# Causal attention: the masked row maximum over two PSUM banks in one instruction, and the exponentials one head at a time

## The chip, the cores and the metric

The kernel runs on one core of a Trainium2 chip. The metric is the device time of one execution in microseconds (us). A core has TensorE (PE, matrix multiplies, with its weight loads shown as PEld), VectorE (DVE), ScalarE (ACT), GpSimd (POOL) and SyncE (SP, which here issues DMAs). Each engine takes its own instructions strictly in order, and semaphores hold an engine back until another has counted far enough. TensorE writes to PSUM, which has eight banks; a bank holds 512 float32 values in each of 128 partitions.

## The reference

The program is two "macaron" layers on `x` of 4 sequences x 1024 tokens x 256 channels. Only the attention of the second layer is touched by the change:

```python
q, k, v = split(x @ w_attn.T + b_attn)            # 16 heads of 16 channels
scores = einsum('bhqd,bhkd->bhqk', q, k) / sqrt(16)
scores = where(mask, scores, -inf)                # causal: k <= q; and (odd, odd - 1) is shut out too
w = softmax(scores, axis=-1)
y = einsum('bhqk,bhkd->bhqd', w, v)
return y @ w_proj.T + b_proj
```

The sequence length is 1024, since the stream `x` is drawn as 4 x 1024 x 256. Before it come two FP4 feed-forward layers, a local attention and a mixture of experts; after it another mixture of experts. None of these is touched.

## The kernel before

`causal_attention` works on "quads": four heads of one sequence, 16 quads in all. Query and key are split into three bf16 parts each, so one product has 96 rows of contraction. A quad needs two passes over its scores.

**Pass one, the row maximum.** For each head and each block of 128 queries (`qb`), the scores of all keys up to the diagonal are multiplied (L2203, `max_scores`) and reduced to one negated maximum per row (L2106 and L2110, `reduce_max`). A bank holds 512 keys, so a block with `qb` of 4 or more takes two steps: the first 512 keys go through a plain `tensor_reduce` (L2110), the rest through a custom instruction that adds the mask and takes the minimum (L2106). `MAX_STEPS` lists the 48 steps of a quad, widest block first. The two partial maxima are joined in `split_max` (L2118). The maxima are then split into two bf16 parts, turned by TensorE (L2210, `turn_max`), copied out by DVE (`store_shift`, L2129) and put under the query rows by two DMAs (L2060).

**Pass two, the exponentials.** For each block of 128 keys (`kb`) and each half `Q` of the queries, TensorE multiplies the scores with the maximum already subtracted (L2226) and adds the mask on the diagonal (L2229); ACT takes the exponential (L2183); TensorE multiplies it with the values in float32 (L2243, `values`). `EXP_SLOTS` lists 24 slots of two heads each. Results of a half are copied by ACT (L2175), turned by TensorE (L2254, `turn_y`) and divided on DVE (L2138, L2140).

**PSUM.** Three banks (`RING = 3`) go round between TensorE and DVE for the steps of pass one and the turned results. Four banks from bank 3 on hold two pairs of heads for ACT. Bank 7 collects the values.

**What sets the order.** Everything is written out by hand. Pass one of the next quad is laid between the slots of pass two: `spread` gives each place (before and after the scores of a slot) steps in proportion to the TensorE columns in that place, up to slot 18 of 24. Two waits tie TensorE to the others: a step of pass one waits until the step `RING` places before it has been emptied (L2202), and the scores of slot `s` wait until the exponential of slot `s - 2` is done (L2222). `values` of four heads are issued after the scores of the slot pair that follows.

Of the kernel before, what the change touches and what calls it, by code (L numbers as in the profile page):

```python
# [15 lines left out]
BF16 = mybir.dt.bfloat16  # L16
# [3 lines left out]
ALU = mybir.AluOpType  # L20
ACT = mybir.ActivationFunctionType
AX_X = mybir.AxisListType.X

P = 128
# [1882 lines left out]
def causal_attention(ch, name):  # L1907
# [9 lines left out]
    nc, ps = ch.nc, ch.ps  # L1917
    RING, EXPB, YB = 3, 3, 7
    QUADS = BATCHES * HEADS // QUAD
# [5 lines left out]
    QB = TPB  # L1925
    MAX_STEPS = [(h, qb, k0, min(512, (qb + 1) * P - k0)) for qb in reversed(range(QB)) for h in range(QUAD)
                 for k0 in range(0, (qb + 1) * P, 512)]
    EXP_SLOTS = [(Q, kb, pair) for Q in range(HALVES) for kb in range(4 * Q + 4) for pair in range(2)]
    NM, NE = len(MAX_STEPS), len(EXP_SLOTS)
    MAX_BY, M_AT, Y0_AT, Y1_AT = 18, 19, 13, 3  # L1930
    NPB = 4
    VW = HD + 1
# [4 lines left out]
    def columns(s):  # L1937

        Q, kb, _ = EXP_SLOTS[s]
        n = 512 - max(0, kb - 4 * Q) * P  # L1940
        return 2 * n + (2 * P if kb >= 4 * Q else 0), (4 * n + 512 if s % 2 else 0)

    def spread(slots):

        places = [(s, i) for s in slots for i in range(2)]
        work = [columns(s % NE)[i] for s, i in places]
        share, at = sum(n for _, _, _, n in MAX_STEPS) / sum(work), {p: [] for p in places}
        p, room = 0, work[0] * share
        for k, (_, _, _, n) in enumerate(MAX_STEPS):
            while room < n / 2 and p + 1 < len(places):  # L1950
                p += 1
                room += work[p] * share
            at[places[p]].append(k)
            room -= n
        return at
# [37 lines left out]
    def place(q, what):  # L1993

        return PLACE[q, what], PLACE[q, what] % RING

    with ExitStack() as ctx:
# [35 lines left out]
        nm = ch.sb(name + "nm", [P, 2, QUAD, QB], ctx=until_y_done)  # L2033
        nm2 = ch.sb(name + "nm2", [P, 2, QUAD, QB], ctx=until_y_done)
        mp = ch.sb(name + "mp", [P, 4, QUAD * QB], BF16, ctx=until_y_done)
        mT = ch.sb(name + "mT", [2 * QUAD * QB, P], BF16, ctx=until_y_done)
        E = ch.sb(name + "E", [P, NPB, 2, 512], ctx=until_y_done)
        yT = ch.sb(name + "yT", [P, 512], ctx=until_y_done)
        forbidden = ch.sb(name + "forbidden", [P, 512], BF16, ctx=until_y_done)
        unread = ch.sb(name + "unread", [P, RING, 512], BF16, ctx=until_y_done)  # L2040
        rden = ch.sb(name + "rden", [P, 4, QUAD], ctx=until_y_done)
# [8 lines left out]
        with nc.Block() as block:  # L2050
            @block.sync
            def _(sp):
# [12 lines left out]
                def step(q, t, c, end):  # L2065

                    place_shift(q, c)
                    if not end:
                        sp.wait_ge(pv_ok, q * NE + 4)
                        sp.sem_inc(ch.fence, 1)  # L2070
                        stack(q + 2, (c + 2) % NQ)
# [24 lines left out]
            def _(dve):  # L2096
# [3 lines left out]
                def reduce_max(q, k):  # L2100
                    h, qb, k0, n = MAX_STEPS[k]
                    at, bank = place(q, k)
                    dve.wait_ge(filled, at + 1)
                    dst = (nm if k0 == 0 else nm2)[:, q % 2, h, qb:qb + 1]
                    if k0 + n == (qb + 1) * P:
                        nc.vector.tensor_tensor_reduce(out=unread[:, bank, 0:n], in0=ps[:, bank, 0:n],  # L2106
                                                       in1=forbidden[:, 512 - n:512], scale=-1.0, scalar=-MASKED,
                                                       op0=ALU.add, op1=ALU.min, accum_out=dst).then_inc(emptied, 1)
                    else:
                        nc.vector.tensor_reduce(dst, ps[:, bank, 0:n], AX_X, ALU.max, negate=True  # L2110
                                                ).then_inc(emptied, 1)
                    if k == NM - 1:
                        split_max(q % 2)

                def split_max(u):
                    nc.vector.drain()
                    far = nm[:, u, :, 4:QB]
                    nc.vector.tensor_tensor(far, far, nm2[:, u, :, 4:QB], ALU.min)  # L2118
                    nc.vector.drain()
                    flat = nm[:, u, :, :].rearrange("p h q -> p (h q)")  # L2120
                    nc.vector.tensor_copy(mp[:, 0, :], flat)
                    nc.vector.drain()
                    nc.vector.tensor_tensor(mp[:, 1, :], flat, mp[:, 0, :], ALU.subtract).then_inc(mp_ok, 1)  # L2123
# [22 lines left out]
                nc.vector.drain()  # L2146
                nc.vector.tensor_copy(forbidden[:, 512 - P:512], ch.mask[:, 0, :])
                nc.vector.drain()
# [19 lines left out]
            def _(act):  # L2168
                def store_y(q, Q):
                    act.wait_ge(pv_ok, q * NE + 12 + 16 * Q)  # L2170
                    if Q:
# [5 lines left out]
                def step(q, t, c, end):  # L2177
                    for s, (Q, kb, pair) in enumerate(EXP_SLOTS):
                        n = 512 - max(0, kb - 4 * Q) * P
                        act.wait_ge(s_ok, q * NE + s + 1)  # L2180
                        act.wait_ge(pv_ok, q * NE + s + 1)
                        bank = EXPB + 2 * (s % 2)
                        nc.scalar.activation(E[:, s % NPB, :, 0:n], ps[:, bank:bank + 2, 0:n], ACT.Exp,  # L2183
                                             scale=float(HD) ** -0.5).then_inc(e_ok, 1)
                        if s == 1 and q:
                            store_y(q - 1, 1)
                        if s == 9:
                            store_y(q, 0)
# [4 lines left out]
            def _(pe):  # L2193
                def max_scores(q, k):

                    h, qb, k0, n = MAX_STEPS[k]
                    c = q % NQ
# [3 lines left out]
                    if at >= RING:  # L2201
                        pe.wait_ge(emptied, at - RING + 1)  # L2202
                    nc.tensor.matmul(ps[:, bank, 0:n], Qs[c][0:STACK, h, qb * P:(qb + 1) * P],  # L2203
                                     Ks[c][0:STACK, h, k0:k0 + n], start=True, stop=True).then_inc(filled, 1)

# [8 lines left out]
                def scores(q, c, s):  # L2214
                    Q, kb, pair = EXP_SLOTS[s]
                    q0 = max(kb * P, Q * 512)
# [5 lines left out]
                    pe.wait_ge(e_ok, q * NE + s + 1)  # L2222
                    for hh in range(2):
                        h = 2 * pair + hh
                        o = ps[:, EXPB + 2 * (s % 2) + hh, :]
                        last = nc.tensor.matmul(o[:, 0:n], Ks[c][:, h, kb * P:(kb + 1) * P],  # L2226
                                                Qs[c][:, h, q0:q0 + n], start=True, stop=not diag)
                        if diag:
                            last = nc.tensor.matmul(o[:, 0:P], ch.identb[:, :], ch.mask[:, 1, :],  # L2229
                                                    start=False, stop=True)  # L2230
                    last.then_inc(s_ok, 1)

                def values(q, c, k):

                    Q, kb, _ = EXP_SLOTS[2 * k]
                    off = max(0, kb - 4 * Q) * P
                    if k == 0:
                        pe.wait_ge(va_ok, q + 1)
                    if kb == 0:
                        pe.wait_ge(y_stored, q * 2 + Q + 1)  # L2240
                    pe.wait_ge(e_ok, q * NE + 2 * k + 4)
                    for h in range(QUAD):
                        last = nc.tensor.matmul(ps[h * WIN:(h + 1) * WIN, YB, off:512],  # L2243
                                                Va[:, c, kb, h * VW:h * VW + WIN],
                                                E[:, (2 * k + h // 2) % NPB, h % 2, 0:512 - off],
                                                start=kb == 0, stop=kb == 4 * Q + 3)
                    last.then_inc(pv_ok, 2)

# [10 lines left out]
                pe.sem_inc(y_stored, 1)  # L2259
                pe.sem_inc(pv_ok, 4)  # L2260
                pe.sem_inc(e_ok, 2)
                for k in range(NM):
# [3 lines left out]
                def step(q, t, c, end):  # L2266
                    for s in range(NE):
# [3 lines left out]
                        for j, k in max_steps(q, s, 1):  # L2271
                            max_scores(j, k)
                        if s % 2 and s > 1:
                            values(q, c, (s - 3) // 2)
                        elif s == 1 and q:
                            values(q - 1, (q - 1) % NQ, NE // 2 - 1)
                        if s == Y1_AT and q:
# [5 lines left out]
                turns(pe, step)  # L2283
                values(QUADS - 1, (QUADS - 1) % NQ, NE // 2 - 1)
                turn_y(QUADS - 1, 1)
# [132 lines left out]
```

## Time and profile before

| | us |
|---|---|
| median of 3 runs (2200.66 to 2204.34) | 2203.64 |
| the profiled execution | 2202.5 |
| its span, first to last instruction | 2200.7 |
| TensorE busy in it | 1868.9 (85%) |
| VectorE busy | 1717.7 (78%) |
| ScalarE busy | 1004.6 (46%) |

The causal attention lies between about 1229 and 1754 us of the span. A period of one quad runs from one turning of the maxima (the only instruction of L2210) to the next. The busy time of TensorE counts each matmul with its way through the array, so that matmuls overlap in it; how long one really holds the engine is read from the start of the next.

### The profile page before, as it was taken

To read this page: it belongs to the slowest core of one execution; us is meant where nothing else is said; L and a number is where in the kernel's file an instruction comes from. 1 tells how busy PE (TensorE), PEld (TensorE's weight loads), DVE (VectorE), ACT (ScalarE), POOL (GpSimd) and SP (SyncE) were. 2 spreads that over 40 slices of the span, in tenths; PEclk is the share of its full clock that TensorE was granted. 3 is DMA by queue.
4 is the path that set the end of the run, shared out by engine and by line. 5 is a ranking of instruction groups with operands and counts; after the bars stand their busy time and mean duration, and the time that the engine had idled before them with its cause. 6 is when DMAs were issued, how large, how long until landed. Compare 5 with 4: busy or idle time off the path is not lost. (4 is left out here: it accounts for less than half of the span.)

```text
span 2200.7 us, 36425 instructions
## 1 busy us (share of the span) xinstructions
PE 1868.9 (85%) x11363; PEld 1353.1 (61%) x11363; DVE 1717.7 (78%) x4040; ACT 1004.6 (46%) x1972; POOL 803.7 (37%) x862
## 2 busy tenths in 40 slices
PE   2799997889999539999978799999999874599998
PEld 1777786778777328787856334444444362487787
DVE  8788984598987568777978788888888366787788
ACT  1333334433332814334556256566666635243345
POOL 2223321133332657886244400000000036688843
PEclk7899997999999659999989699999999986699999
DMA  5000001100000622224425524324432016122256
GB/s 187 1 0 0 0 1 23 35 1 0 0 0 1 206 78 86 89 92 125 153 66 157 103 41 59 48 41 59 59 59 31 2 62 202 45 90 90 92 156 189
DMA packets 112048, 150.28 MB, mean 68 GB/s; under 512 B 19431, under 2 KB 84237, under 8 KB 111373
## 3 DMA queue, kind: packets, MB, share of 16 engines
q1 hardware_dynamic: 95232, 106.53, 20.1%
q0 software_dynamic: 14400, 40.41, 5.9%
q8 instruction: 87, 1.43, 0.3%
q10 hardware_dynamic: 2252, 1.29, 0.2%
q14 instruction: 77, 0.62, 0.1%
HBM read 100.71 MB, written 47.20 MB: 67 GB/s over the span
## 5 line engine op out<-in xcount | busy, mean ns | idle before, releaser
L2183 ACT ACTIVATE t_E<-ps 128x1024 f32<-128x1024 f32 (+3 forms) x384 | 292.6, 813 | 217.9 <-PE ps L2229 164.3
L1569 PE MATMUL ps<-m_w,m_xT 128*128 (+1 forms) x1248 | 348.9, 415 | 1.2 <-DVE m_xT L1649 1.2
L2203 PE MATMUL ps<-t_Ks,t_Qs 96*128 96x512 bf16 (+3 forms) x768 | 234.5, 343 | 19.2 <-PEq L1737 5.7
L2106 DVE CUSTOM_DVE_ANT_0 t_unread<-ps,t_forbidden 128x256 bf16<-128x256 f32 (+3 forms) x512 | 233.8, 486 | 21.3 <-PE ps L2203 19.4
L1569 PEld LDWEIGHTS ps<-m_w,m_xT 128*128 128x128 f32 x1248 | 223.5, 192 | 39.4 <-issue 2.0
L693 PE MATMUL ps<-wdT,f_hT 128*128 128x256 f32 (+1 forms) x768 | 193.2, 394 | 18.2 <-ACT f_hT L735 18.2
L2226 PE MATMUL ps<-t_Qs,t_Ks 98*128 98x512 bf16 (+3 forms) x768 | 199.1, 329 | 3.9 <-DMA t_Qs<-t_mT 2.6
L1587 PE MATMUL ps<-m_w,m_hT 128*128 (+1 forms) x1248 | 200.3, 296 | 0.5 <-DVE m_hT L1666 0.5
L2110 DVE TENSOR_REDUCE t_nm<-ps 128x1 f32<-128x512 f32 x256 | 176.4, 689 | 25.4 <-PE ps L2203 23.8
L192 POOL TENSOR_TENSOR f_h<-f_h,f_hs 128x704 f32<-128x704 f32 x64 | 88.7, 1386 | 276.6 <-DVE f_h L230 276.6
L1621 ACT ACTIVATE m_hT<-ps 128x256 fp32r<-128x256 f32 x208 | 80.1, 385 | 227.5 <-PE ps L1578 227.5
L2091 POOL COPY t_Va<-t_V 128x128 f32<-128x128 f32 x64 | 16.1, 295 | 436.9 <-DVE t_mp L2123 436.6
L2203 PEld LDWEIGHTS ps<-t_Ks,t_Qs 96*128 96x128 bf16 x768 | 72.9, 98 | 166.6 <-DVE t_nm L2106 66.8
L693 PEld LDWEIGHTS ps<-wdT,f_hT 128*128 128x128 f32 (+1 forms) x768 | 137.1, 191 | 60.5 <-ACT f_hT L735 25.7
L1656 DVE TENSOR_TENSOR m_ab<-ps,m_b 128x512 f32<-128x512 f32 x208 | 143.1, 688 | 36.5 <-PE ps L1569 35.5
L2243 PE MATMUL ps<-t_E,t_Va 128*32 128x512 f32 (+3 forms) x1536 | 163.8, 498 | 0.0
L1587 PEld LDWEIGHTS ps<-m_w,m_hT 128*128 128x128 f32 x1248 | 162.4, 191 | 0.9 <-DVE m_hT L1666 0.9
L223 ACT ACTIVATE f_hmagic<-f_h 128x704 f32<-128x704 f32 x64 | 50.8, 793 | 240.7 <-DVE f_h L197 240.7
L1485 POOL DMA_INDIRECT m_picked_out<-m_y,m_dst_row x144 | 143.9, 999 | 42.1 <-issue 32.5
L1475 POOL DMA_INDIRECT m_xg<-m_rows,m_src_row x144 | 140.1, 973 | 50.7 <-issue 34.8
L657 PE MATMUL ps<-wgT,f_xT 128*128 128x352 f32 x768 | 145.5, 340 | 7.4 <-DVE f_h L565 4.5
L657 PEld LDWEIGHTS ps<-wgT,f_xT 128*128 128x128 f32 x768 | 128.0, 197 | 13.7 <-DVE f_xT L558 5.7
(299 smaller groups left out, 3900.2 us busy)
## 6 DMA issues: line engine op xcount, KB each, us to landing
m_raw<-in_L_ffn_rw SPq DMA_DIRECT2D x48, 256.0 KB, 3.2
t_parts<-t_qkv_part SPq DMA_DIRECT2D x64, 192.0 KB, 2.7
t_Qs<-t_parts SPq DMA_DIRECT2D x96, 128.0 KB, 4.1
t_Ks<-t_parts SPq DMA_DIRECT2D x96, 128.0 KB, 6.8
m_yl<-m_picked_out SPq DMA_DIRECT2D x40, 256.0 KB, 3.1
m_rows<-m_xn SPq DMA_DIRECT2D x16, 512.0 KB, 4.2
m_xg<-m_rows SPq DMA_DIRECT2D x64, 128.0 KB, 2.7
m_y<-m_picked_out SPq DMA_DIRECT2D x24, 256.0 KB, 3.1
```

The lines of the kernel that those rows point to most:

```text
L657: last = nc.tensor.matmul(ps[:, bank + half, 0:FH], xT[:, par, kx, c, j * P:(j + 1) * P], w[:, kw, c, half * FH:(half + 1) * FH], start=k ...
L693: last = nc.tensor.matmul(ps[:, DOWN, 0:D], hT[0:rr, r, :], ch.wdT[0:rr, r, :], start=r == 0, stop=r == FC - 1)
L1485: nc.gpsimd.indirect_dma_start(out=picked_out[:, :], out_offset=bass.IndirectOffsetOnAxis(ap=dst_row[:, i:i + 1], axis=0), in_=y[:, i % RI ...
L1569: last = nc.tensor.matmul(ps[:, H1 + u, :], xT[:, u, kx, k, :], of_expert(w1, kw, e, k), start=n == 0, stop=n == 3 * DC - 1)
L1587: last = nc.tensor.matmul(ps[:, OUT + u, 0:D], hT[:, u, kh, f, :], of_expert(w2, kw, e, f), start=n == 0, stop=n == 3 * FK - 1)
L1656: tt(ab[:, u, :], ps[:, H1 + u, :], row_of(b1, e), ALU.add).then_inc(ab_ok, 1)
L2106: nc.vector.tensor_tensor_reduce(out=unread[:, bank, 0:n], in0=ps[:, bank, 0:n], in1=forbidden[:, 512 - n:512], scale=-1.0, scalar=-MASKED ...
L2110: nc.vector.tensor_reduce(dst, ps[:, bank, 0:n], AX_X, ALU.max, negate=True).then_inc(emptied, 1)
L2183: nc.scalar.activation(E[:, s % NPB, :, 0:n], ps[:, bank:bank + 2, 0:n], ACT.Exp, scale=float(HD) ** -0.5).then_inc(e_ok, 1)
L2203: nc.tensor.matmul(ps[:, bank, 0:n], Qs[c][0:STACK, h, qb * P:(qb + 1) * P], Ks[c][0:STACK, h, k0:k0 + n], start=True, stop=True).then_inc ...
L2226: last = nc.tensor.matmul(o[:, 0:n], Ks[c][:, h, kb * P:(kb + 1) * P], Qs[c][:, h, q0:q0 + n], start=True, stop=not diag)
L2243: last = nc.tensor.matmul(ps[h * WIN:(h + 1) * WIN, YB, off:512], Va[:, c, kb, h * VW:h * VW + WIN], E[:, (2 * k + h // 2) % NPB, h % 2, 0 ...
```

## The change

Pass one: a block of queries is one step, 32 in a quad. For `qb` of 4 or more two matmuls fill two neighbouring banks, and one masked instruction reads both. The plain reduction, `nm2` and the joining of partial maxima go. `RING` is 2, each place two banks wide. Pass two: a slot is one head, 48 in a quad, in three single banks (`NEB = 3`); scores of slot `s` wait for the exponential of slot `s - 3`. `values` of heads 4k to 4k+3 come after the scores of slot 4k + 6. The number of exponential buffers stays the same in heads (8).

```diff
-    RING, EXPB, YB = 3, 3, 7
+    RING, EXPB, NEB, YB = 2, 4, 3, 7
-    MAX_STEPS = [(h, qb, k0, min(512, (qb + 1) * P - k0)) for qb in reversed(range(QB)) for h in range(QUAD)
-                 for k0 in range(0, (qb + 1) * P, 512)]
-    EXP_SLOTS = [(Q, kb, pair) for Q in range(HALVES) for kb in range(4 * Q + 4) for pair in range(2)]
+    MAX_STEPS = [(h, qb) for qb in reversed(range(QB)) for h in range(QUAD)]
+    EXP_SLOTS = [(Q, kb, h) for Q in range(HALVES) for kb in range(4 * Q + 4) for h in range(QUAD)]
-    MAX_BY, M_AT, Y0_AT, Y1_AT = 18, 19, 13, 3
-    NPB = 4
+    MAX_BY, M_AT, Y0_AT, Y1_AT = 36, 39, 26, 8
+    NPB = 2 * QUAD
+    LAG = QUAD + 2
...
-        return PLACE[q, what], PLACE[q, what] % RING
+        return PLACE[q, what], 2 * (PLACE[q, what] % RING)
+    def wide(bank, n):
+        return ps[:, bank:bank + 2, :].rearrange("p b n -> p (b n)")[:, 0:n]
...
-                    if k0 + n == (qb + 1) * P:
-                        nc.vector.tensor_tensor_reduce(out=unread[:, bank, 0:n], in0=ps[:, bank, 0:n],
-                                                       in1=forbidden[:, 512 - n:512], scale=-1.0, scalar=-MASKED,
-                                                       op0=ALU.add, op1=ALU.min, accum_out=dst).then_inc(emptied, 1)
-                    else:
-                        nc.vector.tensor_reduce(dst, ps[:, bank, 0:n], AX_X, ALU.max, negate=True
-                                                ).then_inc(emptied, 1)
+                    nc.vector.tensor_tensor_reduce(out=unread[:, at % RING, 0:n], in0=wide(bank, n),
+                                                   in1=forbidden[:, SEQ - n:SEQ], scale=-1.0, scalar=-MASKED,
+                                                   op0=ALU.add, op1=ALU.min, accum_out=nm[:, q % 2, h, qb:qb + 1]
+                                                   ).then_inc(emptied, 1)
...
-                    far = nm[:, u, :, 4:QB]
-                    nc.vector.tensor_tensor(far, far, nm2[:, u, :, 4:QB], ALU.min)
-                    nc.vector.drain()
...
-                        nc.scalar.activation(E[:, s % NPB, :, 0:n], ps[:, bank:bank + 2, 0:n], ACT.Exp,
+                        nc.scalar.activation(E[:, s % NPB, 0:n], ps[:, EXPB + s % NEB, 0:n], ACT.Exp,
                                              scale=float(HD) ** -0.5).then_inc(e_ok, 1)
...
-                    nc.tensor.matmul(ps[:, bank, 0:n], Qs[c][0:STACK, h, qb * P:(qb + 1) * P],
-                                     Ks[c][0:STACK, h, k0:k0 + n], start=True, stop=True).then_inc(filled, 1)
+                    for k0 in range(0, (qb + 1) * P, 512):
+                        n = min(512, (qb + 1) * P - k0)
+                        last = nc.tensor.matmul(ps[:, bank + k0 // 512, 0:n], Qs[c][0:STACK, h, qb * P:(qb + 1) * P],
+                                                Ks[c][0:STACK, h, k0:k0 + n], start=True, stop=True)
+                    last.then_inc(filled, 1)
...
-                    pe.wait_ge(e_ok, q * NE + 2 * k + 4)
+                    pe.wait_ge(e_ok, q * NE + QUAD * k + QUAD + NEB)
...
-                        if s % 2 and s > 1:
-                            values(q, c, (s - 3) // 2)
+                        if s % QUAD == LAG % QUAD and s >= LAG:
+                            values(q, c, (s - LAG) // QUAD)
-                pe.sem_inc(e_ok, 2)
+                pe.sem_inc(e_ok, NEB)
```

Two places show what moves on TensorE. The first is the group of key block 3 in the first half, where a head has 128 query columns. Before (L2226 and L2229 scores and mask, L2203 a step of pass one, L2243 values; in brackets the semaphores waited for, `t_exp` from ACT, `t_emptied` from DVE):

```order
L2226 MATMUL ps<-t_Qs,t_Ks 128x128 [waits t_exp]
L2229 MATMUL ps<-maskb,identb 128x128
L2226 MATMUL ps<-t_Qs,t_Ks 128x128
L2229 MATMUL ps<-maskb,identb 128x128
L2203 MATMUL ps<-t_Ks,t_Qs 128x512 [waits t_emptied]
L2226 MATMUL ps<-t_Qs,t_Ks 128x128 [waits t_exp]
L2229 MATMUL ps<-maskb,identb 128x128
L2226 MATMUL ps<-t_Qs,t_Ks 128x128
L2229 MATMUL ps<-maskb,identb 128x128
L2203 MATMUL ps<-t_Ks,t_Qs 128x256 [waits t_emptied]
L2243 MATMUL ps<-t_E,t_Va 32x256 [waits t_exp]
L2243 MATMUL ps<-t_E,t_Va 32x256 x3
```

The same place in the changed kernel (the lines are now 2224, 2227, 2202 and 2241); the first head of the group that lies between two runs of values is the last one of 256 columns:

```order
L2224 MATMUL ps<-t_Qs,t_Ks 128x256 [waits t_exp]
L2227 MATMUL ps<-maskb,identb 128x128
L2224 MATMUL ps<-t_Qs,t_Ks 128x128 [waits t_exp]
L2227 MATMUL ps<-maskb,identb 128x128
L2224 MATMUL ps<-t_Qs,t_Ks 128x128 [waits t_exp]
L2227 MATMUL ps<-maskb,identb 128x128
L2224 MATMUL ps<-t_Qs,t_Ks 128x128 [waits t_exp]
L2227 MATMUL ps<-maskb,identb 128x128
L2202 MATMUL ps<-t_Ks,t_Qs 128x512 [waits t_emptied]
L2202 MATMUL ps<-t_Ks,t_Qs 128x256
L2241 MATMUL ps<-t_E,t_Va 32x256 [waits t_exp]
L2241 MATMUL ps<-t_E,t_Va 32x256 x3
```

Each head now has a wait of its own, the four heads stand in a row without a step of pass one between them, and the step is one of 768 columns behind the scores.

The second place is the end of a quad's pass one, where the narrow blocks come, ahead of the values of key block 3 in the second half. Before:

```order
L2226 MATMUL ps<-t_Qs,t_Ks 128x512 [waits t_exp]
L2229 MATMUL ps<-maskb,identb 128x128
L2226 MATMUL ps<-t_Qs,t_Ks 128x512
L2229 MATMUL ps<-maskb,identb 128x128
L2203 MATMUL ps<-t_Ks,t_Qs 128x256 [waits t_emptied] x2
L2226 MATMUL ps<-t_Qs,t_Ks 128x512 [waits t_exp]
L2229 MATMUL ps<-maskb,identb 128x128
L2226 MATMUL ps<-t_Qs,t_Ks 128x512
L2229 MATMUL ps<-maskb,identb 128x128
L2203 MATMUL ps<-t_Ks,t_Qs 128x256 [waits t_emptied] x2
L2203 MATMUL ps<-t_Ks,t_Qs 128x128 [waits t_emptied] x4
L2243 MATMUL ps<-t_E,t_Va 32x512 [waits t_exp]
```

The same place in the changed kernel:

```order
L2202 MATMUL ps<-t_Ks,t_Qs 128x384 [waits t_emptied]
L2224 MATMUL ps<-t_Qs,t_Ks 128x512 [waits t_exp]
L2227 MATMUL ps<-maskb,identb 128x128
L2202 MATMUL ps<-t_Ks,t_Qs 128x256 [waits t_emptied]
L2224 MATMUL ps<-t_Qs,t_Ks 128x512 [waits t_exp]
L2227 MATMUL ps<-maskb,identb 128x128
L2202 MATMUL ps<-t_Ks,t_Qs 128x256 [waits t_emptied] x3
L2202 MATMUL ps<-t_Ks,t_Qs 128x128 [waits t_emptied] x2
L2241 MATMUL ps<-t_E,t_Va 32x512 [waits t_exp]
L2241 MATMUL ps<-t_E,t_Va 32x512 x3
L2202 MATMUL ps<-t_Ks,t_Qs 128x128 [waits t_emptied] x2
```

Six narrow steps stood in a row ahead of the values; now five do, and two more come behind the values. Each of them waits for the step two places before it instead of three.

## Rows read from the trace of the kernel before

**Rows 1.** Windows: us, busy PE, PEld, DVE, ACT, POOL (instructions), clock, DMA share, GB/s

```profile
1229.00:1260.00 31.00, 23.96 (x53) 5.54 (x54) 27.60 (x88) 1.28 (x1) 14.10 (x12) 0.50 0.39 57
...
1292.48:1726.20 433.72, 424.71 (x3263) 181.27 (x3260) 366.07 (x1228) 266.10 (x364) 13.05 (x52) 1.00 0.34 49
```

**Rows 2.** Waits, 1260 to 1726 us: who waited for whom, us, times, longest

```profile
PEld ps L2203 <- DVE t_nm L2106: 57.8, 139, 0.8
PEld ps L2226 <- ACT t_E L2183: 8.7, 14, 0.6
```

**Rows 3.** Timeline, PE: start, us, instruction; two turnings of the maxima

```profile
1292.48 0.23 PE L2210 MATMUL ps<-identb,t_mp 128*128 128x128 bf16 x1
...
1726.20 0.23 PE L2210 MATMUL ps<-identb,t_mp 128*128 128x128 bf16 x1
```

**Rows 4.** Timeline, PE, 1431 to 1444 us: the places where steps wait

```profile
1431.11 0.42 PE L2243 MATMUL ps<-t_E,t_Va 128*32 128x128 f32 x8
...
1431.64 0.23 PE L2203 MATMUL ps<-t_Ks,t_Qs 96*128 96x128 bf16 x1
...
1432.80 0.43 PE L2203 MATMUL ps<-t_Ks,t_Qs 96*128 96x128 bf16 x2
...
1433.39 0.23 PE L2203 MATMUL ps<-t_Ks,t_Qs 96*128 96x128 bf16 x1 [0.16 <-DVE t_nm L2110]
...
1439.02 0.87 PE L2203 MATMUL ps<-t_Ks,t_Qs 96*128 96x384 bf16 x3
...
1439.83 0.64 PE L2243 MATMUL ps<-t_E,t_Va 128*32 128x512 f32 x4
...
1442.33 0.60 PE L2203 MATMUL ps<-t_Ks,t_Qs 96*128 96x256 bf16 x3
...
1443.84 1.07 PE L2243 MATMUL ps<-t_E,t_Va 128*32 128x512 f32 x8
```

**Rows 5.** Timeline, DVE and PEld, pass one of the first quad

```profile
1232.44 0.69 DVE L2110 TENSOR_REDUCE t_nm<-ps 128x1 f32<-128x512 f32 x1
...
1233.05 0.68 DVE L2106 CUSTOM_DVE_ANT_0 t_unread<-ps,t_forbidden 128x512 bf16<-128x512 f32 x1
...
1233.66 0.69 DVE L2110 TENSOR_REDUCE t_nm<-ps 128x1 f32<-128x512 f32 x1
...
1233.80 0.10 PEld L2203 LDWEIGHTS ps<-t_Ks,t_Qs 96*128 96x128 bf16 x1 [0.50 <-DVE t_nm L2106]
...
1254.32 0.29 DVE L2106 CUSTOM_DVE_ANT_0 t_unread<-ps,t_forbidden 128x128 bf16<-128x128 f32 x1
...
1254.53 0.29 DVE L2106 CUSTOM_DVE_ANT_0 t_unread<-ps,t_forbidden 128x128 bf16<-128x128 f32 x1
```

**Rows 6.** Timeline, PE and DVE, 1438 to 1446 us: steps filled, a half divided

```profile
1438.14 0.26 DVE L2138 RECIPROCAL t_rden<-ps 128x16 f32<-128x16 f32 x1 [0.43 <-PE ps L2254]
...
1438.81 0.68 DVE L2106 CUSTOM_DVE_ANT_0 t_unread<-ps,t_forbidden 128x512 bf16<-128x512 f32 x1
...
1443.33 0.29 DVE L2106 CUSTOM_DVE_ANT_0 t_unread<-ps,t_forbidden 128x128 bf16<-128x128 f32 x1
...
1444.84 0.39 PE L2203 MATMUL ps<-t_Ks,t_Qs 96*128 96x512 bf16 x1
...
1445.27 0.69 DVE L2110 TENSOR_REDUCE t_nm<-ps 128x1 f32<-128x512 f32 x1 [0.22 <-PE ps L2203]
```

**Rows 7.** Timeline, PE and ACT, the last quad

```profile
1736.71 1.04 PE L2226 MATMUL ps<-t_Qs,t_Ks 98*128 98x512 bf16 x4
...
1737.36 1.94 ACT L2183 ACTIVATE t_E<-ps 128x1024 f32<-128x1024 f32 x2 [0.68 <-PE ps L2226]
...
1739.35 0.61 PE L2226 MATMUL ps<-t_Qs,t_Ks 98*128 98x512 bf16 x2 [0.31 <-ACT t_E L2183]
```

**Rows 8.** Groups by line and shape, 1260 to 1726 us: busy, mean ns, idle before

```profile
L2183 ACT ACTIVATE t_E<-ps 128x512 f32<-128x512 f32 x58 | 31.5, 595 | 38.3 <-PE ps L2229 38.3
...
L2183 ACT ACTIVATE t_E<-ps 128x256 f32<-128x256 f32 x58 | 20.6, 382 | 23.1 <-PE ps L2229 22.1
```

More of the change, by code:

```diff
@@ L1940, in columns @@
         n = 512 - max(0, kb - 4 * Q) * P
-        return 2 * n + (2 * P if kb >= 4 * Q else 0), (4 * n + 512 if s % 2 else 0)
+        return n + (P if kb >= 4 * Q else 0), (4 * n + 512 if s % QUAD == LAG % QUAD else 0)
     def spread(slots):
@@ L1946, in spread @@
         work = [columns(s % NE)[i] for s, i in places]
-        share, at = sum(n for _, _, _, n in MAX_STEPS) / sum(work), {p: [] for p in places}
+        share, at = sum((qb + 1) * P for _, qb in MAX_STEPS) / sum(work), {p: [] for p in places}
         p, room = 0, work[0] * share
-        for k, (_, _, _, n) in enumerate(MAX_STEPS):
+        for k, (_, qb) in enumerate(MAX_STEPS):
+            n = (qb + 1) * P
             while room < n / 2 and p + 1 < len(places):
@@ L2033, in causal_attention @@
         nm = ch.sb(name + "nm", [P, 2, QUAD, QB], ctx=until_y_done)
-        nm2 = ch.sb(name + "nm2", [P, 2, QUAD, QB], ctx=until_y_done)
         mp = ch.sb(name + "mp", [P, 4, QUAD * QB], BF16, ctx=until_y_done)
         mT = ch.sb(name + "mT", [2 * QUAD * QB, P], BF16, ctx=until_y_done)
-        E = ch.sb(name + "E", [P, NPB, 2, 512], ctx=until_y_done)
+        E = ch.sb(name + "E", [P, NPB, 512], ctx=until_y_done)
         yT = ch.sb(name + "yT", [P, 512], ctx=until_y_done)
-        forbidden = ch.sb(name + "forbidden", [P, 512], BF16, ctx=until_y_done)
-        unread = ch.sb(name + "unread", [P, RING, 512], BF16, ctx=until_y_done)
+        forbidden = ch.sb(name + "forbidden", [P, SEQ], BF16, ctx=until_y_done)
+        unread = ch.sb(name + "unread", [P, RING, SEQ], BF16, ctx=until_y_done)
         rden = ch.sb(name + "rden", [P, 4, QUAD], ctx=until_y_done)
@@ L2068, in step @@
                     if not end:
-                        sp.wait_ge(pv_ok, q * NE + 4)
+                        sp.wait_ge(pv_ok, q * NE + NPB)
                         sp.sem_inc(ch.fence, 1)
@@ L2100, in reduce_max @@
                 def reduce_max(q, k):
-                    h, qb, k0, n = MAX_STEPS[k]
+                    h, qb = MAX_STEPS[k]
+                    n = (qb + 1) * P
                     at, bank = place(q, k)
                     dve.wait_ge(filled, at + 1)
-                    dst = (nm if k0 == 0 else nm2)[:, q % 2, h, qb:qb + 1]
-                    if k0 + n == (qb + 1) * P:
-                        nc.vector.tensor_tensor_reduce(out=unread[:, bank, 0:n], in0=ps[:, bank, 0:n],
-                                                       in1=forbidden[:, 512 - n:512], scale=-1.0, scalar=-MASKED,
-                                                       op0=ALU.add, op1=ALU.min, accum_out=dst).then_inc(emptied, 1)
-                    else:
-                        nc.vector.tensor_reduce(dst, ps[:, bank, 0:n], AX_X, ALU.max, negate=True
-                                                ).then_inc(emptied, 1)
+                    nc.vector.tensor_tensor_reduce(out=unread[:, at % RING, 0:n], in0=wide(bank, n),
+                                                   in1=forbidden[:, SEQ - n:SEQ], scale=-1.0, scalar=-MASKED,
+                                                   op0=ALU.add, op1=ALU.min, accum_out=nm[:, q % 2, h, qb:qb + 1]
+                                                   ).then_inc(emptied, 1)
                     if k == NM - 1:
@@ L2146, in _ @@
                 nc.vector.drain()
-                nc.vector.tensor_copy(forbidden[:, 512 - P:512], ch.mask[:, 0, :])
+                nc.vector.tensor_copy(forbidden[:, SEQ - P:SEQ], ch.mask[:, 0, :])
                 nc.vector.drain()
@@ L2169, in store_y @@
                 def store_y(q, Q):
-                    act.wait_ge(pv_ok, q * NE + 12 + 16 * Q)
+                    act.wait_ge(pv_ok, q * NE + NPB + 4 * QUAD + 8 * QUAD * Q)
                     if Q:
@@ L2177, in step @@
                 def step(q, t, c, end):
-                    for s, (Q, kb, pair) in enumerate(EXP_SLOTS):
+                    for s, (Q, kb, _) in enumerate(EXP_SLOTS):
                         n = 512 - max(0, kb - 4 * Q) * P
@@ L2181, in step @@
                         act.wait_ge(pv_ok, q * NE + s + 1)
-                        bank = EXPB + 2 * (s % 2)
-                        nc.scalar.activation(E[:, s % NPB, :, 0:n], ps[:, bank:bank + 2, 0:n], ACT.Exp,
+                        nc.scalar.activation(E[:, s % NPB, 0:n], ps[:, EXPB + s % NEB, 0:n], ACT.Exp,
                                              scale=float(HD) ** -0.5).then_inc(e_ok, 1)
-                        if s == 1 and q:
+                        if s == 3 and q:
                             store_y(q - 1, 1)
-                        if s == 9:
+                        if s == 3 * QUAD + LAG + 1:
                             store_y(q, 0)
@@ L2194, in max_scores @@
                 def max_scores(q, k):
-                    h, qb, k0, n = MAX_STEPS[k]
+                    h, qb = MAX_STEPS[k]
                     c = q % NQ
@@ L2214, in scores @@
                 def scores(q, c, s):
-                    Q, kb, pair = EXP_SLOTS[s]
+                    Q, kb, h = EXP_SLOTS[s]
                     q0 = max(kb * P, Q * 512)
@@ L2222, in scores @@
                     pe.wait_ge(e_ok, q * NE + s + 1)
[L2223 to L2230, printed above, removed]
+                    o = ps[:, EXPB + s % NEB, :]
+                    last = nc.tensor.matmul(o[:, 0:n], Ks[c][:, h, kb * P:(kb + 1) * P],
+                                            Qs[c][:, h, q0:q0 + n], start=True, stop=not diag)
+                    if diag:
+                        last = nc.tensor.matmul(o[:, 0:P], ch.identb[:, :], ch.mask[:, 1, :],
+                                                start=False, stop=True)
                     last.then_inc(s_ok, 1)
                 def values(q, c, k):
-                    Q, kb, _ = EXP_SLOTS[2 * k]
+                    Q, kb, _ = EXP_SLOTS[QUAD * k]
                     off = max(0, kb - 4 * Q) * P
@@ L2244, in values @@
                                                 Va[:, c, kb, h * VW:h * VW + WIN],
-                                                E[:, (2 * k + h // 2) % NPB, h % 2, 0:512 - off],
+                                                E[:, (QUAD * k + h) % NPB, 0:512 - off],
                                                 start=kb == 0, stop=kb == 4 * Q + 3)
-                    last.then_inc(pv_ok, 2)
+                    last.then_inc(pv_ok, QUAD)
                 def turn_y(q, Q):
@@ L2259, in _ @@
                 pe.sem_inc(y_stored, 1)
-                pe.sem_inc(pv_ok, 4)
-                pe.sem_inc(e_ok, 2)
+                pe.sem_inc(pv_ok, NPB)
+                pe.sem_inc(e_ok, NEB)
                 for k in range(NM):
@@ L2272, in step @@
                             max_scores(j, k)
-                        if s % 2 and s > 1:
-                            values(q, c, (s - 3) // 2)
-                        elif s == 1 and q:
-                            values(q - 1, (q - 1) % NQ, NE // 2 - 1)
+                        if s % QUAD == LAG % QUAD and s >= LAG:
+                            values(q, c, (s - LAG) // QUAD)
+                        elif s == LAG % QUAD and q:
+                            values(q - 1, (q - 1) % NQ, NE // QUAD - 1)
                         if s == Y1_AT and q:
@@ L2283, in _ @@
                 turns(pe, step)
-                values(QUADS - 1, (QUADS - 1) % NQ, NE // 2 - 1)
+                values(QUADS - 1, (QUADS - 1) % NQ, NE // QUAD - 1)
                 turn_y(QUADS - 1, 1)
```

## The prediction

> **What bounds the kernel now.** I read the windows first, then the waits, then the timeline of TensorE. In the steady stretch (1292 to 1726 us) the clock is full, TensorE shows 425 busy us of 434 and VectorE 366 [rows 1]. Fourteen quads pass between the two turnings, 433.72 us, so a quad takes 30.98 us [rows 3]. The reader should not trust the 98%: the real hold of a matmul is columns divided by 2.4 per ns, since starts in a row lie that far apart. The waits view shows whom TensorE waits for: its steps of pass one wait 139 times for the masked instruction of DVE, its scores only 14 times for ACT [rows 2]. Put against the columns, four places of a quad are real stalls [rows 4]. From 1442.33 to 1443.84 two steps of 256 and four of 128 columns stream 0.43 us and the change to float32 values takes 0.10, so 0.98 is waiting; 1432.80 to 1433.39 holds 0.27 of streaming, 0.32 waiting; 1439.02 to 1439.83 holds 0.48 + 0.10, 0.23 waiting; values of 128 columns take 0.36 and the next step starts 0.53 later, 0.17 waiting. Together 1.70 us; the other 29.3 us of a quad are TensorE's own work. The bound is TensorE, plus a hand-over to DVE.
>
> **Numbers for the hand-over.** A DVE read of 512 columns gives way to the next after 0.61 us in both forms, one of 128 after 0.21 [rows 5]: 0.08 us fixed and 1.04 ns a column. TensorE starts 0.14 us after the read that it waited for [rows 5]. A step of 512 streams 0.21 us and is read 0.43 us after its start, so 0.22 us pass between stream and reader [rows 6]. With these figures the traced cluster comes out: its first step of 128 is read from 1443.33 [rows 6], ends 1443.54, the fourth, three places on, starts 0.14 later at 1443.68, and 0.05 + 0.10 us later values begin: 1443.83, traced 1443.84 [rows 4]. For ACT: two matmuls of 512 from 1736.71 end at 1737.14 and the exponential starts at 1737.36, again 0.22; the two exponentials end at 1739.30 and the score that waited starts at 1739.35 [rows 7]. An exponential of 512 elements takes 0.595 us, of 256 0.38 [rows 8]; by that line 0.49 for 384 and 0.28 for 128. A masked block adds 0.06 us of TensorE.
>
> **What goes.** TensorE multiplies the same columns. DVE loses 16 reads a quad at 0.08 us fixed, 1.2 us, and the joining of the maxima, about 0.2. Those are worth something only where TensorE waits for DVE. Wide reads are not in the trace: by the line 1024 columns take 1.14, 896 1.01, 768 0.88, 640 0.74. At worst they cost what two reads do (1.22 for 1024), at best the fixed part is free (1.06); I take the line, since 128 to 512 lie on it.
>
> **What comes on the ACT side.** Behind a waiting score stand all of TensorE's later work and so DVE's steps. The fourth head after a run of values now needs the exponential of the first head after it, where before it needed a head four back, which was done during the values. From the start of the first to the start of the fourth must pass: stream, 0.22, exponential, 0.05.
> - First head 256 columns, then three of 128 (twice a quad): 0.17 + 0.22 + 0.38 + 0.05 = 0.81 needed, TensorE has 0.17 + 0.12 + 0.12 = 0.41. Stall 0.40, twice.
> - Masked 512, then three of 384 (first half): 0.28 + 0.22 + 0.60 + 0.05 = 1.15, against 0.74. Stall 0.41.
> - 384, the turning of the maxima, three of 256 (second half): 0.98 against 0.63. Stall 0.35.
> - Four of 512 with a step of 640 between (twice): 1.08 against 0.94. Stall 0.14, twice.
>
> In the other groups a wide step or a turning stands between and covers it. Sum 1.84 us, near zero before.
>
> **What comes on the DVE side.** A step now waits for the one two places back. In units of the wide steps: stream, 0.22, read, 0.14 must fit between a step and the next but one.
> - Behind the turning of the maxima: 0.43 + 0.22 + 1.14 + 0.14 = 1.93, and TensorE, its ACT wait included, has 1.59. Stall 0.35.
> - A turned half takes one of the two places. Step 7 (896 columns): 0.37 + 0.22 + 1.01 + 0.14 = 1.74, TensorE has 1.43 up to the step behind the turning. Stall 0.3. For the other half DVE divides for 0.67 us [rows 6] and three steps behind it wait 0.2, 0.15 and 0.45: 0.8.
> - The last steps of 640 and first of 512: 0.1.
> - The narrow cluster. Let the first 256 start at 0; the last 384 is read until 0.41. The first 256 is read 0.41 to 0.75. The second starts at 0.41 + 0.14 = 0.55, is there at 0.88 and read until 1.22; the third starts 0.89, read until 1.56; the fourth starts 1.36, read until 2.03; the first 128 starts 1.70, read until 2.24; the second starts 2.17, and values at 2.33. Without waits TensorE would be there at 0.91: stall 1.4 against 0.98 before. It is worse although DVE does the same reads, because two places leave DVE idle while TensorE refills.
>
> Sum 2.95 against 1.70. The old waits at 1431 to 1440 do go; the new ones are dearer.
>
> **Sum.** A quad gains 1.84 + 2.95 - 1.70 = 3.1 us. Fourteen steady quads 43.4, the first, between the other two kinds, 3. Pass one of the first quad runs at a granted clock of 0.50, the level of 1.2 GHz, bound by DVE [rows 1]: the reads save 1.2 and the joining 0.2, but with two places the loop of two steps is 0.14 + columns/1.2 + 0.22 + read, which passes two reads at every width, by 0.04 (1024) to 0.13 us (128) a step; four heads times 0.65 is 2.6. Net +1.1. The last quad has no steps; its groups lengthen by 0.1 to 0.4 and one gets shorter: +1. Together 48.5. The profiled execution took 2202.5 us, 1.1 below the median of the runs, so 2251 by its own time and 2252 beside the median.
>
> Two ideas of the skill pull apart here. The Trainium skill, Advanced Engine Details and Errata, TRN2 Errata (The Read-Write Bubble), advises tiles of 512 or 1024 elements, as ScalarE and VectorE pay a latency between instructions; by it DVE's side gets cheaper and ACT's dearer. The rows agree on the size: 0.08 us a read. The Trainium skill, Perfetto Trace Analysis, Optimization Strategy, reads a gap that repeats on the engine that should be full as too few buffers; by it, going from three places to two and from four heads to three makes the time rise, which is my forecast. The sum above needs neither sentence.
>
> **Rivals.**
> 1. *The saved reads pay (faster).* DVE is busy 84% of the steady stretch [rows 1] and TensorE waits for it; with 1.4 us less a quad and wide steps TensorE would find its place free. If all old waits go and none come: 15 x 1.70 + 1.4 = 27, 2175. Against: the hand-over of a wide step is longer than the work between. It decides if a quad's waits end below 1.70. Chance 0.08. The errata rule above, taken alone, asks for this one.
> 2. *Only the ring costs.* If one-bank exponentials come back soon enough: 1.25 x 15 + 2 = 21, 2224. Against: each needed time is made of traced durations. 0.15.
> 3. *Only the exponentials cost*, the wider steps paying for the lost place: 1.84 x 15 + 1 = 29, 2232. 0.07.
> 4. *Wide reads at the price of two, in places where TensorE waits*: another 1.2 a quad, 2270. 0.12.
> 5. Nothing moves, as losses and gains cancel: 2204. 0.03.
>
> That the change misses its aim in the code is out: the order shows the steps as described.
>
> **How the numbers follow.** My case has 0.55, own range 2240 to 2262. Within 0.2% (about 4.4 us) no change can be told. Slower is my case and rivals 2 to 4: 0.89; same 0.03; faster 0.08. The range from 2222 to 2272 leaves out rivals 1 and 5 and the edges of 2 and 4, under 0.2.
>
> **What would show it.** The period between turnings should be 34 us, not 31. Scores should wait for ACT six times a quad, 0.1 to 0.4 us. Steps behind a turning and in the narrow cluster should wait for DVE, 1.4 us in the cluster. DVE's busy time should fall by more than 1 us a quad and ACT's rise, TensorE's clock stay full. A period of 31 or less, or scores without waits, makes me wrong.

## The result, and the profile after

The changed kernel takes 2254.49 us (median of 4 runs, 2253.16 to 2256.36) against 2202.15 us of the kernel before, run beside it: a ratio of 1.023 with a 95% interval of 1.0218 to 1.0241. The forecast was 2252 us. The profiled execution took 2253.16 us with a span of 2251.4.

The answer to [rows 3], the turnings of the maxima on TensorE's timeline (start in us, duration, instruction):

```profile
1258.34 0.29 PE L2210 MATMUL ps<-identb,t_mp 128*128 128x128 bf16 x1 [0.93 <-DVE t_mp L2121]
...
1294.58 0.22 PE L2210 MATMUL ps<-identb,t_mp 128*128 128x128 bf16 x1
...
1773.59 0.22 PE L2210 MATMUL ps<-identb,t_mp 128*128 128x128 bf16 x1
```

Fourteen quads pass between the last two: 479.01 us, so 34.21 a quad against 30.98. That is 45.3 us of the 50.7 by which the span grew. The windows of these stretches answer to [rows 1] (us, busy PE, PEld, DVE, ACT, POOL, clock, DMA share, GB/s):

```profile
1229.00:1260.00 31.00, 21.00 (x49) 4.01 (x49) 27.01 (x70) 1.28 (x1) 14.29 (x12) 0.50 0.34 51
...
1294.58:1773.59 479.01, 448.44 (x3261) 170.75 (x3260) 351.17 (x992) 297.95 (x700) 13.08 (x52) 1.00 0.32 44
```

The clock of the steady stretch is full as before. DVE's busy time fell from 26.1 to 25.1 us a quad (84% of it before, 73% now); ACT's rose from 19.0 to 21.3, which in the longer quad is 62% after 61%. Neither is at its limit. What grew is waiting. The waits view, 1296 to 1770 us, answers to [rows 2] (who waited for whom, us in total, times, longest):

```profile
PEld ps L2202 <- DVE t_nm L2109: 75.3, 180, 0.8
PEld ps L2224 <- ACT t_E L2180: 70.3, 152, 0.8
```

Scores waited 14 times for ACT before; now 152 times. These figures still contain time in which TensorE streamed something older. To take that out, each matmul's columns/2.4 ns (and 0.10 us more ahead of values) were subtracted, as in the prediction, from the time between its start and the start of the next; what is left was summed over a quad (median of nine quads). Below this is called "by the starts". Before: steps 1.65 us, scores 0. After: steps 2.91, scores 1.83, together 4.74. The difference, 3.09, is nearly all of the 3.23 us by which the quad grew.

The group of the first diff place shows the wait for ACT, on the timeline of TensorE and ACT:

```profile
1468.29 0.28 PE L2224 MATMUL ps<-t_Qs,t_Ks 98*128 98x256 bf16 x1
...
1468.59 0.22 PE L2224 MATMUL ps<-t_Qs,t_Ks 98*128 98x128 bf16 x1
1468.65 0.22 PE L2227 MATMUL ps<-maskb,identb 128*128 128x128 bf16 x1
1468.67 1.04 ACT L2180 ACTIVATE t_E<-ps 128x256 f32<-128x256 f32 x4 [1.45 <-PE ps L2227]
...
1469.11 0.23 PE L2224 MATMUL ps<-t_Qs,t_Ks 98*128 98x128 bf16 x1 [0.24 <-ACT t_E L2180]
```

The first head of 256 columns starts at 1468.29, the fourth of the group at 1469.11: 0.82 us, where 0.81 was worked out. The third head's mask began at 1468.65 and took 0.06, so 0.40 us were lost.

The narrow cluster (the steps of 256 and 128 columns at the end of a quad's pass one), in answer to the last two of [rows 4], on the timeline of TensorE:

```profile
1493.36 0.27 PE L2202 MATMUL ps<-t_Ks,t_Qs 96*128 96x256 bf16 x1
...
1493.90 0.63 PE L2202 MATMUL ps<-t_Ks,t_Qs 96*128 96x256 bf16 x2
...
1494.71 0.57 PE L2202 MATMUL ps<-t_Ks,t_Qs 96*128 96x256 bf16 x2 [0.18 <-DVE t_nm L2109]
...
1495.52 0.23 PE L2202 MATMUL ps<-t_Ks,t_Qs 96*128 96x128 bf16 x1 [0.23 <-DVE t_nm L2109]
...
1495.68 1.07 PE L2241 MATMUL ps<-t_E,t_Va 128*32 128x512 f32 x8
```

From the first 256 to the values 2.32 us pass; the working gave 2.33, of which 1.4 is waiting.

### The profile page after: what moved, and what is told of

It reads as the page before. It is cut to its first block and busy times, and to the rows that moved or that the text cites. A ratio compares the mean times of both kernels' runs of the same rounds, so it can differ in the third digit from the quotient of the medians.

```text
span 2251.4 us, 36905 instructions
## 1 busy us (share of the span) xinstructions
PE 1890.9 (84%) x11363; PEld 1337.8 (59%) x11363; DVE 1704.5 (76%) x3768; ACT 1040.5 (46%) x2356; POOL 804.2 (36%) x862
## 3 DMA queue, kind: packets, MB, share of 16 engines
q10 hardware_dynamic: 2252, 1.29, 0.2%
## 5 line engine op out<-in xcount | busy, mean ns | idle before, releaser
L2109 DVE CUSTOM_DVE_ANT_0 t_unread<-ps,t_forbidden 128x256 bf16<-128x256 f32 (+7 forms) x512 | 372.3, 756 | 123.5 <-PE ps L2202 117.1
L2180 ACT ACTIVATE t_E<-ps 128x512 f32<-128x512 f32 (+3 forms) x768 | 328.4, 494 | 232.2 <-PE ps L2227 173.8
L2202 PE MATMUL ps<-t_Ks,t_Qs 96*128 96x512 bf16 (+3 forms) x768 | 215.0, 342 | 31.6 <-DVE t_nm L2109 23.1
L2224 PE MATMUL ps<-t_Qs,t_Ks 98*128 98x512 bf16 (+3 forms) x768 | 214.0, 331 | 18.4 <-ACT t_E L2180 14.9
L2224 PEld LDWEIGHTS ps<-t_Qs,t_Ks 98*128 98x128 bf16 x768 | 72.8, 97 | 148.5 <-ACT t_E L2180 91.5
L2202 PEld LDWEIGHTS ps<-t_Ks,t_Qs 96*128 96x128 bf16 x768 | 63.0, 98 | 159.9 <-DVE t_nm L2109 105.6
```

What stands on the lines that cost most here:

```text
L2109: nc.vector.tensor_tensor_reduce(out=unread[:, at % RING, 0:n], in0=wide(bank, n), in1=forbidden[:, SEQ - n:SEQ], scale=-1.0, scalar=-MASK ...
L2180: nc.scalar.activation(E[:, s % NPB, 0:n], ps[:, EXPB + s % NEB, 0:n], ACT.Exp, scale=float(HD) ** -0.5).then_inc(e_ok, 1)
L2202: last = nc.tensor.matmul(ps[:, bank + k0 // 512, 0:n], Qs[c][0:STACK, h, qb * P:(qb + 1) * P], Ks[c][0:STACK, h, k0:k0 + n], start=True, ...
```

## The experiments

**The exponential half alone, three banks.** Pass one is that of the kernel before (three places, steps of at most 512), pass two that of the changed kernel:

```diff
-    RING, EXPB, YB = 3, 3, 7
+    RING, EXPB, NEB, YB = 3, 3, 3, 7
...
-    EXP_SLOTS = [(Q, kb, pair) ... for pair in range(2)]
+    EXP_SLOTS = [(Q, kb, h) ... for h in range(QUAD)]
...
```

> The exponential half of the change alone: one head a slot in three banks, while pass one stays as before (steps of at most 512 columns, three places). Theory (the fourth head after the values waits for the exponential of the first, about 2.0 us a quad, and the ring of three keeps its 1.7): a quad takes 33.0 to 33.3 us instead of 31.0, the kernel 2230 to 2236 us. Rival (the loss is all in the ring of two places): 2200 to 2208 us.

2227.69 us, ratio 1.011 (1.0086 to 1.0134); a quad takes 32.50 us:

```profile
1615.13 0.22 PE L2210 MATMUL ps<-identb,t_mp 128*128 128x128 bf16 x1
...
1647.63 0.22 PE L2210 MATMUL ps<-identb,t_mp 128*128 128x128 bf16 x1
```

The rival falls, but the expected size was some 0.6 us a quad too high. By the starts, scores wait 1.38 us a quad and steps 1.55. In three groups, of 256 and 128 columns, the waits are 0.13, 0.19 and 0.19 us instead of the 0.35, 0.41 and 0.41 of the changed kernel. With 48 steps instead of 32, a step of 512 columns stands between the heads of each of these groups, where the changed kernel has none, and each wait is shorter by 0.22 us, about what such a step streams (0.21). So the price of three banks depends on what stands between the heads. The other half of the change alone, wide steps with pairs of heads, was not run: it would take four banks, four banks and the one for the values, nine where there are eight.

**The same with four banks.** One number:

```diff
-    RING, EXPB, NEB, YB = 3, 3, 3, 7
+    RING, EXPB, NEB, YB = 3, 3, 4, 7
```

> As the run with three banks for single heads, but with four (the eighth bank is free when pass one keeps three): the same 768 exponentials, one place more. Theory (depth is what counts): the waits of scores for ACT nearly vanish, a quad takes 30.8 to 31.3 us, 2198 to 2208 us. Rival (twice the number of exponentials is what costs, by its fixed part on ACT): as slow as with three banks, about 2230 us or more.

2208.09 us, ratio 1.002 (1.0009 to 1.0031); a quad takes 31.23 us:

```profile
1602.75 0.22 PE L2210 MATMUL ps<-identb,t_mp 128*128 128x128 bf16 x1
...
1633.98 0.22 PE L2210 MATMUL ps<-identb,t_mp 128*128 128x128 bf16 x1
```

Scores wait no longer (0 us by the starts). So 768 exponentials instead of 384 cost 0.2% and the missing fourth head some 20 us more: the depth is what costs.

**The changed kernel with its four banks given out by the bank.** A wide step takes two, a narrow one or a turned result one; the wait is for the last user of the bank:

```diff
-        return PLACE[q, what], 2 * (PLACE[q, what] % RING)
+        return PLACE[q, what], BANK[PLACE[q, what]]
...
-                    if at >= RING:
-                        pe.wait_ge(emptied, at - RING + 1)
+                    if BEFORE[at] >= 0:
+                        pe.wait_ge(emptied, BEFORE[at] + 1)
...
```

> The changed kernel with its four banks of pass one given out by the bank: a step of more than 512 columns takes two neighbouring ones, every other step and every turned result takes one, so narrow steps are four deep. Theory: the narrow cluster's waits fall from 1.4 to about 0.5 us, the three waits behind the second turned half go (0.6), those behind the turning of the maxima and behind the first turned half stay; 1.5 us a quad, 2229 to 2236 us. Rival (the wide reads themselves are what TensorE waits for, not the number of places): within 5 us of the changed kernel, 2250 to 2255 us.

2227.83 us, ratio to before 1.0104 (1.0079 to 1.013), some 27 us below the changed kernel and a little below the expected 2229; a quad takes 32.65 us:

```profile
1590.10 0.22 PE L2225 MATMUL ps<-identb,t_mp 128*128 128x128 bf16 x1
...
1622.75 0.22 PE L2225 MATMUL ps<-identb,t_mp 128*128 128x128 bf16 x1
```

Waits of steps fall from 2.91 to 1.22 us: in the cluster to 0.42, behind the second turned half to nothing, while those behind the turning of the maxima (0.34) and the first turned half (0.40) stay as expected. Scores still wait 1.97. The number of places explains the step side: the wide reads are still there, and all but 1.22 us of the waits are not.

**Two places, nothing else.** The kernel before with one number changed:

```diff
-    RING, EXPB, YB = 3, 3, 7
+    RING, EXPB, YB = 2, 3, 7
```

> The kernel before with RING = 2 and nothing else: single-bank steps of at most 512 columns, two places. Theory: two places leave DVE idle while TensorE refills in the narrow cluster and behind every turned result; at least the 1.2 us a quad that the ring costs the changed kernel, 2222 to 2250 us. Rival (two places are enough, since DVE's reads take longer than a refill): 2202 to 2208 us.

2269.24 us, ratio 1.0291 (1.0264 to 1.0317). The direction is as expected, the time lies 19 us above the expected range; a quad takes 34.69 us:

```profile
1621.63 0.23 PE L2210 MATMUL ps<-identb,t_mp 128*128 128x128 bf16 x1
...
1656.32 0.23 PE L2210 MATMUL ps<-identb,t_mp 128*128 128x128 bf16 x1
```

Steps wait 5.24 us. Some 13 of the 65 us fall in the first quad and its pass one, the rest in the steady quads. The 1.2 us that I had taken from the changed kernel is a net figure: there the wide instruction has paid a part back, as the next run shows. With narrow steps the lost place by itself is dearer than the whole change.

**The changed kernel without the wide instruction.** Single heads in three banks, two places, steps of at most 512. Against the first experiment one number differs:

```diff
-    RING, EXPB, NEB, YB = 3, 3, 3, 7
+    RING, EXPB, NEB, YB = 2, 3, 3, 7
```

> The changed kernel without the wide instruction: one head a slot in three banks, two places, but steps of at most 512 columns in single banks as before (the plain and the masked form). It tells what merging two reads is worth by itself. Theory (a wide step gives DVE more work for each hand-over, so two places leave it less idle): slower than the changed kernel; if the loss of two places (65 us in the run with RING = 2) and that of three banks (23 us) simply add, 2285 to 2295 us, so that the merging gives back some 35 us. Rival (merging saves only its 16 fixed parts of 0.08 us a quad, where TensorE waits): at most 20 us slower than the changed kernel, below 2274 us.

2292.61 us, ratio 1.0407 (1.0385 to 1.0429); 23 us of the heads and 65 of the places simply add, as expected. A quad takes 36.13 us:

```profile
1594.90 0.22 PE L2210 MATMUL ps<-identb,t_mp 128*128 128x128 bf16 x1
...
1631.03 0.22 PE L2210 MATMUL ps<-identb,t_mp 128*128 128x128 bf16 x1
```

The changed kernel is 38 us faster than this. So between two places the wide step is a gain, 1.9 us a steady quad and some 10 us in the first quad with its pass one; that is more than the 1.2 us of fixed time that DVE saves a quad. A wide step gives DVE more to read while the other place is refilled, which fits, but it also holds two banks instead of one, and the two were not parted: four places of one bank with narrow steps, which eight banks would hold, were not run. With more places the wide step gave nothing: wide steps with banks given out one by one take 2227.83 us, narrow steps in three banks beside the same three heads 2227.69.

**Does the order of the steps give back the waits?** The kernel before, blocks mixed:

```diff
-    ... for qb in reversed(range(QB)) for h in range(QUAD)
+    ... for qb in (7, 0, 6, 1, 5, 2, 4, 3) for h in range(QUAD)
```

> The kernel before with the blocks of queries of pass one in the order 7, 0, 6, 1, 5, 2, 4, 3 instead of widest first, nothing else. Theory (the narrow steps cost TensorE because they stand together at the end of a quad, 0.98 us, and at 1428 to 1434 us, 0.5 us, where DVE needs longer for a step than TensorE gives it): between wide steps they are covered, waits of steps fall from 1.65 to about 0.5 us a quad, 2180 to 2192 us. Rival (DVE is the bound of the stretch, so that its waits only move): within 5 us of before, 2199 to 2207 us.

2200.01 us, ratio 0.9988 (0.9979 to 0.9997). A miss: a quad takes 30.75 us and steps still wait 1.38. The four heads of a block still come in a row, so four steps of 128 stand together. Waits of 0.09 and 0.31 us also stand ahead of steps of 512. The same order with one head a slot and four banks:

> The same mixed order together with one head a slot in four banks. Theory: waits of steps about 0.5 us a quad, none of scores; 2184 to 2196 us, no better than the mixed order alone, since the single heads gave nothing with four banks. Rival (finer slots let the mixed steps spread better): below 2180 us.

2198.75 us, ratio 0.9976 (0.9965 to 0.9986): the fastest here, but by 5 us only, and so a miss of the expected range too. To part the narrow steps for good, blocks were then paired head by head:

```diff
-    ... for qb in reversed(range(QB)) for h in range(QUAD)
+    ... for two in ((7, 0), (6, 1), (5, 2), (4, 3)) for h in range(QUAD) for qb in two
```

> The kernel before with pass one ordered head by head in pairs of blocks (7, 0), (6, 1), (5, 2), (4, 3), so that each narrow step stands between wide ones; in the run with the blocks alone mixed the four heads of a block still came in a row. Theory (narrow steps in a row are what waits): waits of steps about 0.5 us a quad instead of 1.65 (before) and 1.38 (blocks mixed), a quad 29.8 to 30.1 us, 2182 to 2192 us. Rival (what is left are waits that the order of steps cannot move: turned results and the fixed time of each hand-over): 1.2 us or more stay, 2196 to 2202 us.

2203.62 us, ratio 1.0 (0.999 to 1.0011); a quad takes 30.93 us, steps wait 1.51:

```profile
1603.66 0.23 PE L2210 MATMUL ps<-identb,t_mp 128*128 128x128 bf16 x1
...
1634.59 0.23 PE L2210 MATMUL ps<-identb,t_mp 128*128 128x128 bf16 x1
```

My theory fell here; of the rival the 1.2 us or more that stay came true, and its range of times lies just below the measured one. The cluster is gone, but waits of 0.05 to 0.38 us stand ahead of steps of 384 and 512 instead. And with single heads in four banks:

> The same order with one head a slot in four banks. Theory: as with pairs of heads, within 4 us of that run, since scores wait in neither. Rival: the finer slots let steps lie more evenly, 5 us or more faster.

2203.43 us, ratio 1.0 (0.9988 to 1.0011): the same, as the theory had it. With three places the waits of steps moved and did not go. Where they would go with more places can't be told from these runs.

## Why the prediction was right

*TensorE's own work is constant.* 34.21 us less 4.74 of waiting is 29.5; before, 30.98 less 1.65 is 29.3. Right.

The mechanism holds, for the sums and for the single waits; the agreement of the total to 2.5 us also has some luck in it, at the two ends.

*The reads.* The wide read is on the line of the narrow ones. From the first quad's pass one on DVE's timeline:

```profile
1233.39 1.22 DVE L2109 CUSTOM_DVE_ANT_0 t_unread<-ps,t_forbidden 128x1024 bf16<-128x1024 f32 x1
...
1234.54 1.22 DVE L2109 CUSTOM_DVE_ANT_0 t_unread<-ps,t_forbidden 128x1024 bf16<-128x1024 f32 x1
...
1252.14 0.55 DVE L2109 CUSTOM_DVE_ANT_0 t_unread<-ps,t_forbidden 128x384 bf16<-128x384 f32 x1
...
1252.82 0.56 DVE L2109 CUSTOM_DVE_ANT_0 t_unread<-ps,t_forbidden 128x384 bf16<-128x384 f32 x1
...
1253.30 0.56 DVE L2109 CUSTOM_DVE_ANT_0 t_unread<-ps,t_forbidden 128x384 bf16<-128x384 f32 x1
```

1024 columns take 1.15 us (1233.39 to 1234.54), forecast 1.14, and the median from start to next start is 1.15 us too for the 54 reads of the steady stretch; two banks in one read cost nothing extra. Rival 4 is out. The rows of 384 columns show the rhythm of two places: 0.68 us to the next read, then 0.48, a gap of 0.20 behind every second read, 0.10 a step as worked out.

*The ACT side.* Forecast 1.84 us a quad, measured 1.83. Wait by wait a steady quad has 0.35, three of 0.40 to 0.41 and two of 0.14, as worked out, and a seventh of 0.06. The runs with three and four banks show that depth is the cause.

*The DVE side.* Forecast 2.95, measured 2.91. Behind the turning of the maxima 0.35 was worked out and 0.35 is waited, behind the first turned half 0.3 and 0.41, behind the second 0.8 and 0.72, in the cluster 1.4 and 1.38. Rival 1 had DVE's saved time as the gain. DVE's busy time did fall, by 1.07 us a quad, and the wide form is worth 38 us between two places. It did not reach the 65 us that the lost place costs, so that rival named a true effect and had the sum wrong. Rivals 2 and 3 each left out one of two real costs.

*The ends.* Pass one of the first quad grew from 23.7 to 25.0 us (first read to the turning), +1.3, forecast +1.1. Two terms were mis-sized and cancel, which is luck. The first quad was taken at +3 and took 36.24 us against 36.34. Its windows, after and then before:

```profile
1258.34:1294.58 36.24, 31.39 (x194) 11.61 (x194) 25.54 (x72) 18.45 (x40) 2.01 (x8) 0.89 0.28 45
```

```profile
1256.14:1292.48 36.34, 32.62 (x192) 12.46 (x193) 27.38 (x90) 17.21 (x21) 2.01 (x8) 0.85 0.33 45
```

By the starts its waits at the full clock grew by 0.9 us only, from 3.4 to 4.3. And the mean clock of 0.89 against 0.85 means that about 8 us of it ran at the lower level (0.50) instead of 11; by an estimate from these rows that gave back up to half of the 3 us, 1.5. Whether the change shortened that stretch is open: in the other runs it ends 7 to 14 us after the first turning.

The last quad was taken at +1 and took 3.5 us longer, 31.05 against 27.58. Its windows, after, before, and in the run with single heads in four banks:

```profile
1773.59:1804.64 31.05, 27.38 (x227) 9.76 (x225) 1.58 (x5) 24.10 (x60) 0.00 (x0) 1.00 0.01 2
```

```profile
1726.20:1753.78 27.58, 25.40 (x229) 9.81 (x225) 1.58 (x5) 21.34 (x32) 0.00 (x0) 1.00 0.01 2
```

```profile
1727.12:1755.69 28.57, 25.67 (x227) 10.01 (x225) 1.58 (x5) 23.77 (x60) 0.00 (x0) 1.00 0.01 2
```

No step of pass one stands there to cover a wait: by the starts, scores and values wait 5.7 us against 2.4 before. ACT is busy for nearly as long with four banks as with three (23.77 and 24.10 us), and yet the quad is 2.5 us shorter; with three banks for the heads and nothing else changed (the first experiment) it is as long as in the changed kernel. So some 2.5 of the 3.5 us are the missing fourth head and 1.0 the single heads themselves; all that my term had for both was 1.

The Trainium skill, Perfetto Trace Analysis, Optimization Strategy, takes a repeating gap on the engine that should be full as a possible sign of too few buffers; the runs with two against three places and three against four banks agree, at 65 and 20 us. The Trainium skill, Perfetto Trace Analysis, Optimizing Scalar/DVE Operations, says that breaking up instructions may let work finish sooner where Scalar or Vector are not saturated but cause bubbles on other engines. Before the change ACT caused none (scores waited 0 us by the starts), so the rule promised nothing here, and with the depth kept at four heads the split exponentials gave nothing (ratio 1.002). The section on the read-write bubble that the prediction cites from the Trainium skill gives no time for one read, so the rows cannot agree with it on the size; the 0.08 us a read is the rows' own.

## What to carry to other kernels

Before an instruction is merged or split, write down for each buffer ring how long a place is held (fill, latency, read, release) and how much work the producer has until it needs the place again; the difference is the stall. For the changed kernel, whose order of work had been followed step by step, sums of such differences met the trace to a few per cent. Carried over to another order without redoing them they failed: 2.0 us for 1.38 in the first experiment, and the waits that the reordering was to remove. Count depth in the unit of work that is handed over, not in banks: four banks were two places, and three banks were three heads where four had been. Busy time saved on a consumer pays only as far as the ring lets the producer run ahead.

## What the runs showed that I had not expected

Taking one of three places away alone cost 65 us (5.24 us of waiting a quad against 1.65), more than the whole change. And reordering the steps removed the waits that the trace named (0.98 us in the narrow cluster) without a gain of more than 0.25%, since most of it came up again at other steps.
